# A scan with a fourth buffer of states, the sums one state later, and two buffers of u^T in place of three

## What is computed

```python
xs, z = jnp.split(h @ in_w, 2, axis=-1); xs = jax.nn.silu(xs)
proj = xs @ xproj_w
dt = jax.nn.softplus(proj[..., :512] + dt_bias)
Bm, Cm = proj[..., 512:576], proj[..., 576:]
def step(hst, ins):                     # for every token t
    dA  = jnp.exp(dt_t[:, :, None] * A)
    hst = hst * dA + (dt_t * x_t)[:, :, None] * B_t[:, None, :]
    y_t = jnp.einsum('bds,bs->bd', hst, C_t)
y = ys + xs * Dskip
return y * jax.nn.silu(z) @ out_w
```

## Time and profile before

| | us |
|---|---|
| median of 3 runs (3501.53 to 3503.8) | 3501.54 |
| the profiled execution | 3503.94 |
| its span in the trace | 3502.2 |
| PE busy in the span | 3332.4 (95%) |
| DVE, ACT, POOL busy | 2982.3, 2901.7, 2303.9 |

### The profile page before, as it was taken

One profiled execution on the slowest core, in us unless ns is written; L12 is line 12 of the kernel. 1 busy time (PEld: TensorE's weight loads), 2 busy tenths in 40 slices (PEclk: granted clock), 3 DMA queues, 4 the chain that ended last, 5 costly groups with the idle time before them and its releaser, 6 DMA issues.

```text
span 3502.2 us, 59842 instructions
## 1 busy us (share of the span) xinstructions
PE 3332.4 (95%) x22946; PEld 2572.1 (73%) x22946; DVE 2982.3 (85%) x2916; ACT 2901.7 (83%) x4667; POOL 2303.9 (66%) x1066
## 2 busy tenths in 40 slices
PE   7999999999999999999999999999899989999999
PEld 5888988898888888988988898898786432222244
DVE  4988999999989999998999999899996578888241
ACT  6999999999999999999999999999985337777620
POOL 1878998898898889988988888899775000000000
PEclk9999999999999999999999999999999989999999
DMA  3223222222222222222222222222211151210000
GB/s 113 73 70 78 79 69 69 62 68 69 65 89 67 69 63 70 74 65 62 79 69 64 67 69 69 62 64 74 72 61 42 44 116 21 37 26 12 0 6 18
DMA packets 193183, 214.19 MB, mean 61 GB/s; under 512 B 75617, under 2 KB 144993, under 8 KB 192641
## 3 DMA queue, kind: packets, MB, share of 16 engines
q1 hardware_dynamic: 192898, 210.36, 20.9%
HBM read 192.19 MB, written 18.06 MB: 60 GB/s over the span
## 4 chain that ended last, share of the span: by engine, by line
PE 75%; ACT 14%; DVE 7%; issue 3%; POOL 1%; DMA 0%; SPq 0%; DVEq 0%; ACTq 0%; POOLq 0%
PE psum L1521 20%; PE psum L1299 18%; PE psum L1515 15%; PE psum L1512 12%; ACT arena L957 5%; ACT arena L940 4%; PE psum L1608 3%; PE psum L1597 3%; DVE arena L1205 2%; PE psum L1572 2%; DVE row_max L1252 2%; PE psum L1541 1%; DVE skip_w L1278 1%; ACT L957 1%; POOL arena L704 1%
## 5 line engine op out<-in xcount | busy, mean ns | idle before, releaser
L720 POOL TENSOR_TENSOR arena<-arena 128x1024 f32<-128x1024 f32 x1024 | 2236.8, 2193 | 409.1 <-DVE arena L1205 386.4
L1205 DVE TENSOR_TENSOR_SCAN arena<-arena,psum 128x512 f32<-128x512 f32 x2048 | 2378.1, 1230 | 148.3 <-PE psum L1515 82.8
L957 ACT ACTIVATE arena<-arena,a_neg 128x512 f32<-128x512 f32 x2048 | 1421.7, 713 | 57.0 <-PE psum L1515 56.2
L1521 PE MATMUL psum<-ident,arena 128*128 128x128 f32 x8192 | 1245.5, 275 | 1.6 <-POOL arena L720 1.6
L940 ACT ACTIVATE arena<-arena,bT 128x512 f32<-128x512 f32 x1536 | 1095.0, 713 | 0.0
L1515 PE MATMUL psum<-ident,arena 128*128 128x128 f32 x6144 | 1021.2, 276 | 0.0
L1521 PEld LDWEIGHTS psum<-ident,arena 128*128 128x128 f32 x8192 | 975.3, 143 | 2.1 <-POOL arena L720 2.1
L1512 PE MATMUL psum<-arena 128*128 128x128 f32 x4096 | 846.8, 289 | 82.2 <-DVE arena L1205 75.8
L1512 PEld LDWEIGHTS psum<-arena 128*128 128x128 f32 x4096 | 654.8, 193 | 320.4 <-issue 189.5
L1515 PEld LDWEIGHTS psum<-ident,arena 128*128 128x128 f32 x6144 | 753.9, 144 | 0.0
L1299 PE MATMUL psum<-arena 128*128 128x512 f32 x1472 | 705.1, 601 | 12.9 <-issue 5.0
(11 more groups left out here) (118 smaller groups left out, 1078.8 us busy)
## 6 DMA issues: line engine op xcount, KB each, us to landing
arena<-bc_dram SPq DMA_DIRECT2D x256, 512.0 KB, 3.7
arena<-diag_dram SPq DMA_DIRECT2D x224, 128.0 KB, 2.1
arena<-qk_dram SPq DMA_DIRECT2D x96, 128.0 KB
diag_dram<-arena SPq DMA_DIRECT2D x32, 256.0 KB, 4.4
qk_dram<-arena SPq DMA_DIRECT2D x12, 512.0 KB, 4.9
arena<-in_x SPq DMA_DIRECT2D x4, 512.0 KB, 10.4
arena<-in_up_w SPq DMA_DIRECT2D x1, 2048.0 KB, 11.7
out_xT<-arena SPq DMA_DIRECT2D x8, 256.0 KB, 2.3
```

What stands on the lines that cost most here:

```text
L720: pool.tensor_tensor(out[:, :, way], h_now[:, :, way], c_row, ALU.mult)\
L957: act.activation(decay[:, w % AHEAD, f], dt_[:, u % 2, f], ACT.Exp, scale=a_neg[:, d, f, st:st + 1])\
L1205: dve.tensor_tensor_scan(hs[:, w % RING, f, rows][:, way], decay[:, w % AHEAD, f, way], psum[:, 4 + n % U_BANKS, way], end_state(w - DS, f ...
L1521: return pe.matmul(psum[:, c, f * P:(f + 1) * P], hs[:, w % RING, f, at:at + P], ident[:, :], is_transpose=True, start=False, stop=w % DS ...
```

## The change

`RING` goes from 3 to 4: `hs` gets a fourth buffer, in the place from which the third buffer of `uT` (two tiles of it) and the scratch `tmp` have moved. `tmp` now lies where that third `uT` buffer was. A new constant `LATER = 3` sets how many states the sums of PE stand behind its turns; it was a literal 2. With it the gate of DVE goes from state 1 to state 2 of a unit, and the first `yT` from state 3 to state 4, which moves every step of `TURN` up to the last `zs` by one state in units 1 to 6, and all of them in unit 7. `bc` and what follows stay, and so do the silu and the softplus of ACT. ACT now waits, in front of the second decay of state w, until PE has turned all of state w-1. The decays keep three buffers. The slide of the scans in their buffers follows `RING`.

```diff
-RING = 3
+RING = 4
+LATER = 3
...
-        uT = [cut(at, TB - DIAGS, DI) for at in (R_UT, R_UT + (TB - DIAGS) * DI, R_XS + NI * HALF)]
+        uT = [cut(at, TB - DIAGS, DI) for at in (R_UT, R_UT + (TB - DIAGS) * DI)]
...
-        hs = cut(R_UH, RING, NI, HALF + SLIDE)
+        hs = [cut(R_UH + k * NI * (HALF + SLIDE), NI, HALF + SLIDE) for k in range(RING - 1)] + [cut(R_UT + 4096, NI, HALF + SLIDE)]
...
                 if step[0] == "yT":
-                    st = max(st, 3)
+                    st = max(st, LATER + 1)
...
-                if w >= AHEAD:
-                    act.wait_ge(s["u_full"], NI * (w - AHEAD + 1))
+                if w >= 2:
+                    act.wait_ge(s["u_full"], NI * (w - 1))
                 if c >= DIAGS:
-                    act.activation(uT[w % AHEAD][:, c - DIAGS], dtxT[:, u % 2, c], ACT.Copy, scale=bT[:, u % 2, c, st:st + 1])\
+                    act.activation(uT[w % 2][:, c - DIAGS], dtxT[:, u % 2, c], ACT.Copy, scale=bT[:, u % 2, c, st:st + 1])\
...
-                        if u and st == 1:
+                        if u and st == LATER - 1:
                             gate_y(u - 1, f)
...
-            for w in range(SCAN_TILES + 2):
+            for w in range(SCAN_TILES + LATER):
...
-                    if w >= 2:
-                        (reduce_state if (w - 2) % DS else first_state)(w - 2, f)
+                    if w >= LATER:
+                        (reduce_state if (w - LATER) % DS else first_state)(w - LATER, f)
```

More of the change, by code:

```diff
@@ L69, in sem @@
             return ctx.enter_context(nc.semaphore(name))
-        arena = sb("arena", [P, 48904])
+        arena = sb("arena", [P, 48896])
         def cut(at, *dims):
@@ L88, in build @@
         R_XS, R_DT, R_DTX, R_ZS = 13824, 17920, 22016, 26112
-        R_DA, R_UH, R_C, R_UT, R_TMP = 28160, 34304, 40712, 42760, 46856
+        R_DA, R_UH, R_C, R_UT, R_TMP = 28160, 34304, 40640, 42688, 15872
         R_BC = 42544
@@ L508, in end_state @@
             at = scan_at(w) + (0 if unit(w // DS)[0] else HALF - 1)
-            return hs[:, w % RING, f, at:at + 1]
+            return hs[w % RING][:, f, at:at + 1]
         block = ctx.enter_context(nc.Block())
@@ L716, in _ @@
                         pool.wait_ge(s["scan_done"], NI * w + f + NI // 2)
-                        h_now = hs[:, w % RING, f:f + NI // 2, scan_at(w):scan_at(w) + HALF]
-                        out = hs[:, w % RING, f:f + NI // 2, prod_at(w):prod_at(w) + HALF]
+                        h_now = hs[w % RING][:, f:f + NI // 2, scan_at(w):scan_at(w) + HALF]
+                        out = hs[w % RING][:, f:f + NI // 2, prod_at(w):prod_at(w) + HALF]
                         c_row = c_rows[:, p % 2, w % 2, way].unsqueeze(1).to_broadcast([P, NI // 2, HALF])
@@ L1204, in _ @@
                         way = slice(None, None, -1) if d else slice(None)
-                        dve.tensor_tensor_scan(hs[:, w % RING, f, rows][:, way], decay[:, w % AHEAD, f, way],
+                        dve.tensor_tensor_scan(hs[w % RING][:, f, rows][:, way], decay[:, w % AHEAD, f, way],
                                                psum[:, 4 + n % U_BANKS, way],
@@ L1514, in turn_u @@
                     else:
-                        o = pe.transpose(dst[:, c * P:(c + 1) * P], uT[w % AHEAD][:, c - DIAGS, f * P:(f + 1) * P], ident[:, :])
+                        o = pe.transpose(dst[:, c * P:(c + 1) * P], uT[w % 2][:, c - DIAGS, f * P:(f + 1) * P], ident[:, :])
                 o.then_inc(s["u_full"], 1)
@@ L1520, in turn_h @@
                 at = prod_at(w) + c * P
-                return pe.matmul(psum[:, c, f * P:(f + 1) * P], hs[:, w % RING, f, at:at + P], ident[:, :],
+                return pe.matmul(psum[:, c, f * P:(f + 1) * P], hs[w % RING][:, f, at:at + P], ident[:, :],
                                  is_transpose=True, start=False, stop=w % DS == DS - 1 and f == NI - 1)
```

## The result

The changed kernel takes 3561.84 us (median of 4 runs, 3561.31 to 3562.68) against 3501.53 (4 runs, 3500.89 to 3503.8). The ratio is 1.0173, with a 95% interval of 1.0157 to 1.0188. It is slower by 60.3 us, and 3.2 us over the 3558.6 of the forecast. The span of the profiled execution went from 3502.2 to 3559.5, by 57.3 us, and the forecast of the span's growth was 57.1. The total was right, but two of its terms were not, as the table further down shows.

A forecast was written before the change was run, and what follows sets the result against it. PE, DVE and ACT, within 8% of each other, were taken to bound the kernel together. Silu 32.4, softplus 17.0, units 7 and 0 7.7 and 0 for the rest gave 57.1 us, so 3558.6; own range 3546 to 3572, with rivals 3530 to 3582.

The forecast's parts named there:

- Bound and mechanism: PE, DVE and ACT all near the bound; ACT's lead absorbs its two blocks, and losing it makes DVE stop on decays.
- those waits at 95 to 105 us: Sign to look for: DVE's waits for ACT's decays rise from 48.4 us to some 95 to 105.
- Ring and lag: Fourth buffer and later sums over the whole scan: 0 us, with bounds of -8.0 and +1.8.
- the working of the end of the scan: Behind the last turn: one added state of sums, 1.8 us, hidden by PE's 1.6 us of waiting for POOL.
- Plain states: ACT's earlier limit outside its blocks: 0 us, as a reserve of 1.2 us holds the copies; upper bound 24 us.
- Rival (b)'s first half: Plain states: the 1.2 us reserve doesn't hold the copies, up to 24 us more; (b) as a whole 3580, chance 0.13.
- The silu after state 33: Units 1 to 6: decay 2.9 us later plus 2.5 of slow clock, 5.4 each, 32.4 us in all.
- rival (a): Behind the silus: the same stops without the fall of the clock, 42 us slower, 3544; chance 0.16.
- Unit 0 has no lead to lose, 0: Silu after state 33 in unit 0: ACT has no lead before it, so the change costs 0 us there.
- the rule that the prediction quoted from the Trainium skill: Behind the silus: transposes do not bring PE to full clock, so no clock loss, 15 us lower, 3543.6.
- The softplus after state 48: Units 0 to 6: 2.4 us of useful lead lost in each, 17.0 us in all, bounds 5 and 35.
- Units 7 and 0: Unit 7's silus 2.2 and 3.2 us, unit 0's first square root 2.3; together 7.7 us, between 0 and 14.

The follow-up runs named there:

- e3_wait_later: The changed kernel with ACT's wait for the turns of state w-1 one decay later in units 1 to 7; 3549.39 us, 1.0138 of the kernel before.
- e1_wait_two: The kernel before with only ACT's wait changed: ahead of state w's second decay it waits for PE's turns of w-1, not w-2; 3559.39 us, 1.0164.
- e4_c_shift: The changed kernel with only addresses moved: C's rows by 2 floats (8 bytes), everything behind them by 4 floats; 3554.36 us, 1.0151.
- e11_pitch: The kernel before with a pitch of 536 floats, not 534, for hs tiles and C's rows on a multiple of 16 bytes; 3504.64 us, 1.0012.

## Why the prediction was right, and where it was not

**Bound and mechanism.** Right, and shown by the wait alone. The lead of ACT pays for its blocks, and without it DVE stops on decays. I expected those waits at 95 to 105 us, and they came to 127.0. Read by stretches of states, all units together, those waits rose by 33.5 us in states 33 to 36 and by 19.6 in 48 to 51, as the blocks want it. They also rose by 14.9 us in states 5 to 32 and by 9.6 in 37 to 47, nearly all in the even units, and units 1 to 6 lost only 1.5 us there: DVE waited for a decay in place of something else (its waits for turns and for sums fell by 13.7 and 5.0 in all). My 95 to 105 had left these out. A rise of a wait is no sum of losses.

**Ring, lag, plain states.** Ring and lag: 0 forecast, and nothing that the times can tell in the run with the lag at two. The scans' waits for sums fell by 5.0 of their 6.4 us. But the working of the end of the scan missed a gain. It had PE's 1.6 us of waiting for POOL hide 1.8 us of extra sums. In the traces with `LATER = 3` those sums kept PE at work, the clock fell for 6.8 us no more, and the stretch became 2.1 us shorter (1.1 in `e3_wait_later`). Plain states: 0 forecast, 1.5 us in units 1 to 6 of the change, 1.7 of the wait alone. Rival (b)'s first half falls.

**The silu after state 33.** The term that was off: 22.1 us against 32.4. Its stop was nearly right (15.9 us in six units, 2.5 to 2.8 each, against 2.9), its clock was not (6.2 us in all, 0 to 1.4 each, against 2.5). The windows of the changed kernel (busy us of PE, its weight loads, DVE, ACT and POOL, then the granted clock): from the first decay behind the silu to the turns of state 36 in unit 2, and the low stretches behind the silus of units 1 and 3:

```profile
915.26:929.65 14.39, 12.05 (x89) 10.27 (x90) 13.04 (x12) 14.05 (x23) 10.27 (x5) 1.00 0.17 50
587.90:591.30 3.40, 3.40 (x12) 2.37 (x11) 3.07 (x3) 3.40 (x6) 2.53 (x2) 0.50 0.00 0
1246.70:1250.10 3.40, 2.96 (x11) 2.44 (x12) 3.40 (x4) 3.40 (x7) 1.69 (x1) 0.50 0.00 0
```

In unit 2 the stretch took 14.39 us against 13.90 and the clock stayed at 1.00. In the five other units it was at 0.50, 1.2 GHz in place of 2.4, for 3.4 us and not for the 6.8 of unit 0. The units lost 4.1, 2.5, 4.2, 3.7, 3.8 and 3.7 us where 5.4 stood. Two assumptions were wrong in that term. PE's stop did not grow by as much as DVE's: PE stopped for 3.0 to 3.6 us in these six units, not for 4.5. And I took the whole low stretch of unit 0 as the price of any such stop. In the five traces that have the shorter lead and this block whole (the change and `e1_wait_two` to `e4_c_shift`) units 1 to 6 have thirty such stops of 3.0 to 3.6 us. Behind four the clock stayed at 1.00, and the unit lost 2.4 to 2.6 us, which is rival (a). Behind 22 it fell for 3.4 us, and behind four for 6.8: in three of the four the unit lost 5.0 to 5.4 us, the price of the forecast, and in `e3_wait_later` 4.4.

"Unit 0 has no lead to lose, 0" came out (0.0 in its states 33 to 36), but not by its reason. DVE's stop on the decay rose there too, from 3.97 to 6.17 us, PE's stop stayed at 3.03, and the clock, which had fallen for 6.8 us before, did not fall in the changed kernel's trace. In the traces of the four runs named above, where it fell for 3.4 us, these states cost 0.7 to 0.8.

By the rule that the prediction quoted from the Trainium skill, "TensorE: Matmul & The Clock Gate", Part 4, the clock would have nothing to lose behind these silus. The 0.50 of five units speaks against it. The 1.00 of the earlier trace rows does so less than the prediction made of it, since 63 of the 87 matmuls that start in that stretch are transposes, not nearly all. But the window 2734.30:2739.30 above holds transposes alone, and it has 1.00 for 5 us.

**The softplus after state 48.** 17.3 against 17.0. The deduction of the 1.72 us that ACT waited for a `dt` tile was right: that wait is gone.

**States 52 and 53.** Not in the forecast: 9.3 us, 0.3 to 1.9 a unit. PE's waits for POOL at L1382 of the changed kernel sum to 16.7 us, against 14.1 before, and the clock falls behind six of the seven, against one. The prediction took the buffers' new places as free. The change moved the pitch of `hs` from 534 to 528 floats, and so made both tiles of a product the slow kind in odd units and at state 50 of even ones. `e4_c_shift` shows that these places matter: the same program with C's rows 8 bytes off takes the item from +9.3 to -1.5. They are not all of it, since `e1_wait_two`, whose products kept their length, lost 3.8 there, and `e11_pitch`, whose products are slow, lost 2.1. How many of the waits the clock falls behind decides the size, and why it falls behind one and not behind another stays open.

**Units 7 and 0.** 7.9 against 7.7, but split 4.2 in unit 7, where 5.4 stood, and 3.7 in unit 0, where 2.3 stood. Behind its state 4 unit 7 lost 5.8 us, 2.5 up to state 32 and 3.3 behind it, near the 2.2 and 3.2 of the working; the rest of the difference is the clock's fall at its start. (Four times 4.7 and 0.7 make 19.5, not 19.6, which changes nothing here.)

So the total was so close by luck: the term of the silu was too large by 10.3 us, 8.8 of them in its clock, and a term of 9.3 us was missing. The mechanism and the softplus term were right by themselves.

## What to carry to other kernels

Before taking a buffer away, ask which engine runs ahead on it and what stretches of other work that lead pays for: the one state of lead that the third buffer of u^T gave was worth under 2 us in plain states and 58 us in all, 39 of them in the four states behind each block. If the buffer must go, the blocks have to shrink first, and a new small block elsewhere costs about its own length again. When buffers move, compare the durations of every instruction that reads them, since a place in memory can cost more than the order does.

## What the hardware showed

**POOL's two-input product depends on 8 bytes.** A product of 128x1024 floats took 2001 ns, 2187 or 2384 (medians in an odd unit), by whether C's rows and the tiles of `hs` lie alike or 8 bytes apart within 16, with one tile each way in the middle case. In even units of the changed kernel 2.00 and 2.37 us alternate in groups of eight states, and in `e11_pitch` in groups of six. The program moves the scans of even units by one float every `RING` states, four here and three there, so a group is two such steps, 8 bytes: the pattern is the same rule. The mean over all units of the changed kernel is 2295 ns.

**The clock's fall after a stop is not one price.** Of thirty PE stops of 3.0 to 3.6 us four left the granted clock at 1.00, 22 were followed by 3.4 us at 0.50 and four by 6.8 us. Stops of the same 3.03 us are in all three groups, so the length of the stop does not decide it. Shorter stops can bring a fall too: behind PE's seven waits of 2.2 to 2.6 us for dt*x it fell six times in the change, seven times in `e3_wait_later`, and once in `e11_pitch`. There is one trace for each kernel, and what decides stays open. Behind the softplus, with a stop of 6.44 us, the window of the changed kernel reads:

```profile
669.80:676.60 6.80, 4.71 (x21) 4.41 (x22) 6.05 (x5) 6.80 (x12) 3.52 (x2) 0.50 0.07 19
```
